# Four modulation rows computed among the first convolutions, and six buffers for the weight quantising

## The reference, cut to what matters

```
mod = (silu(c) @ wmod).reshape(1, 6, 1, 512)
sa, ca, ga, sb, cb, gb = six vectors of 512
ga = sign(ga) * max(|ga|, 0.25);  gb = the same of gb
h  = layernorm(x) * (1 + ca) + sa
x  = x + ga * mamba(h)          # W_in 2048x512, conv of 4 taps, silu, scan over 8192 tokens, 16 states, W_out 512x1024
h  = layernorm(x) * (1 + cb) + sb
x  = x + gb * ffn(h)            # gate, up 1408x512, down 512x1408; weights and inputs in blocks of 16, FP4
```

## Time and profile before

| what | us |
|---|---|
| median of 3 runs (5562.43 to 5564.1) | 5562.72 |
| the profiled execution's own time | 5563.82 |
| its span | 5561.9 |
| busy in the span: PE, DVE | 4831.9, 4961.6 |
| busy in the span: POOL, ACT | 4007.7, 3027.0 |
| end of setup (start of the Mamba block) | 51.13 |
| start of the first scan | 182.80 |

### The profile page before, as it was taken

One profiled execution on the slowest core, in us unless ns is written; L12 is line 12 of the kernel. 1 busy time (PEld: TensorE's weight loads), 2 busy tenths in 40 slices (PEclk: granted clock), 3 DMA queues, 4 the chain that ended last, 5 costly groups with the idle time before them and its releaser, 6 DMA issues. The chain is left out here.

```text
span 5561.9 us, 76495 instructions
## 1 busy us (share of the span) xinstructions
PE 4831.9 (87%) x21860; PEld 3350.4 (60%) x21860; DVE 4961.6 (89%) x4365; ACT 3027.0 (54%) x6492; POOL 4007.7 (72%) x1968
## 2 busy tenths in 40 slices
PE   6688897888978879888897888975799999999999
PEld 3355555455545545545554555554688888888887
DVE  6899999999999999999999999998688888888887
ACT  1677677777777767777677777764211111111111
POOL 4899999999999999999999999998122222222221
PEclk8799999999999999999999999997899999999999
DMA  5455564555545555455565656544210110101100
GB/s 200 155 189 167 179 195 160 189 173 180 191 156 190 176 170 197 159 189 169 178 195 154 193 172 181 184 154 133 93 34 28 34 33 29 34 29 34 34 28 27
DMA packets 398953, 745.63 MB, mean 134 GB/s; under 512 B 44563, under 2 KB 44691, under 8 KB 398454
## 3 DMA queue, kind: packets, MB, share of 16 engines
q1 hardware_dynamic: 394230, 724.19, 40.1%
q0 software_dynamic: 4352, 17.30, 0.9%
HBM read 698.06 MB, written 43.26 MB: 133 GB/s over the span
## 5 line engine op out<-in xcount | busy, mean ns | idle before, releaser
L644 POOL TENSOR_TENSOR slot<-du,b_row 128x1024 f32<-128x1024 f32 x1024 | 2401.4, 2371 | 50.3 <-PE y_ps L1064 45.9
L948 DVE TENSOR_TENSOR_SCAN decays<-decays,state,slot 128x1024 f32<-128x1024 f32 x592 | 1388.5, 2346 | 54.7 <-ACT slot L820 53.3
L811 ACT ACTIVATE decays<-delta,rate 128x512 f32<-128x512 f32 x2048 | 1326.3, 679 | 32.3 <-issue 9.5
L1064 PEld LDWEIGHTS y_ps<-ident,slot 128*128 128x128 f32 x8192 | 1004.9, 149 | 327.5 <-issue 214.0
L1064 PE MATMUL y_ps<-ident,slot 128*128 128x128 f32 x8192 | 1096.2, 287 | 82.2 <-POOL slot L651 78.7
L948 DVE TENSOR_TENSOR_SCAN slot<-decays,state,slot 128x1024 f32<-128x1024 f32 x432 | 1011.5, 2341 | 71.6 <-ACT slot L820 69.7
L651 POOL TENSOR_TENSOR slot<-slot,c_row 128x1024 f32<-128x1024 f32 x432 | 1023.9, 2370 | 69.8 <-ACT state L798 68.2
L1314 POOL TENSOR_TENSOR hq<-hid,qinv 128x1408 f32<-128x1408 f32 x64 | 165.9, 2593 | 1220.5 <-DVE qinv L1340 1220.5
L1004 PE MATMUL work_ps<-h_t,win 128*128 128x512 f32 x2048 | 1000.8, 635 | 35.2 <-DVE delta L874 18.6
L954 DVE TENSOR_TENSOR slot<-decays,c_row 128x1024 f32<-128x1024 f32 x592 | 724.0, 1223 | 56.9 <-DVE decays L948 4.2
L1279 ACT ACTIVATE act_gate<-gate_ps 128x512 f32<-128x512 f32 (+1 forms) x192 | 108.2, 563 | 1136.7 <-PE gate_ps L1421 612.5
(11 more groups left out here) (193 smaller groups left out, 7424.5 us busy)
## 6 DMA issues: line engine op xcount, KB each, us to landing
b_row<-b_c_rows SPq DMA_DIRECT2D x1024, 256.0 KB, 3.8
c_row<-b_c_rows SPq DMA_DIRECT2D x1024, 256.0 KB, 3.6
win<-in_w_in SPq DMA_DIRECT2D x256, 256.0 KB, 4.4
xt<-in_x SPq DMA_DIRECT2D x16, 1024.0 KB, 7.4
xr<-in_x SPq DMA_DIRECT2D x64, 256.0 KB, 4.3
x_after_mamba<-xr SPq DMA_DIRECT2D x64, 256.0 KB, 4.1
xa<-x_after_mamba SPq DMA_DIRECT2D x64, 256.0 KB, 2.8
xres<-x_after_mamba SPq DMA_DIRECT2D x64, 256.0 KB, 2.6
```

The lines of the kernel that those rows point to most:

```text
L644: pool.tensor_tensor(slot[:, u % SLOTS, :, :], du[:, p % 2, :, :], two(b_row[:, u % BC_RING, :]), ALU.mult).then_inc(S["ub_ready"], 1)
L811: act.activation(decay[u % 2][:, i, :], delta[:, p % 2, i, :], ACT.Exp, scale=rate[:, 2 * p + i, n:n + 1]).then_inc(S["decay_ready"], 1)
L948: dve.tensor_tensor_scan(d if u in DVE_C else h, d, h, state[:, 2 * p, n:n + 1], ALU.mult, ALU.add).then_inc(S["scan_done"], 1)
L1064: op = pe.matmul(y_ps[i][:, s, :], slot[:, u % SLOTS, i, s * P:(s + 1) * P], ident[:, :], is_transpose=True, start=False, stop=(n == N - 1 ...
```

## The change

The setup keeps only what the first LayerNorm and the projections need: a third of `wmod`, the two column vectors, `diag`, `rate`, `wdt`. `xc`, which held nothing before the block began, is allocated earlier and its second half serves as home of the rows. The other four modulation vectors are computed in chunk -1 of the Mamba block: SP loads their parts of `w_mod` into buffers that are not in use yet (`delta`, `b_row`, `c_row`, `du`) and `wout` behind them; PE does one 512-column matmul of a row product after each of the 16 `i` and `c` pieces, ACT copies each finished row out after the fourth, eighth, twelfth and sixteenth piece, and DVE makes the signed rows inside `prepare()`, before groups 4 and after group 9. The column of `gb` is made by four small matmuls on PE in place of the way through HBM. `wout` is multiplied by `ga` on POOL at the end of `prepare()`, in four instructions of 1024 elements a partition. The first two groups of feed-forward weights are loaded at the Mamba block's start and the next four at the start of `prepare()`; the ring has six buffers, the two new ones in `zs`.

```diff
-    PREP_RING = SLOTS // 2
+    PREP_RING = SLOTS // 2 + 2
...
-                wmod = ssb("wmod", [P, KT, 6 * DM])
+                wmod = ssb("wmod", [P, KT, 2 * DM])
...
-                LOADS += [(mod_loaded[i], wmod[:, :, pairs[i]], w_mod[:, :, pairs[i]]) for i in range(3)]
+                LOADS += [(mod_loaded, wmod[:, :, :], w_mod[:, :, 0:2 * DM])]
...
-                        pool.wait_ge(mod_loaded[2], 16)
-                        for g in range(PREP_RING):
-                            prep_load(pool, g)
...
-                        for j in range(NB):
-                            dve.tensor_tensor(wout[:, j, :], wout[:, j, :], ga_mag[:, :], ALU.mult)
...
+            VECTORS = (("gate", 5, delta[:, :, :, :].rearrange("p a b t -> p (a b) t")), ("shift", 3, b_row[:, :, :]),
+                       ("scale", 4, c_row[:, :, :]), ("mix", 2, du[:, :, :, :].rearrange("p a b t -> p (a b) t")))
...
+                    load_vector(0)
+                    for i in range(WIN_RING):
+                        load_win(i, Chunk(None, 0))
+                    for i in range(1, len(VECTORS)):
+                        load_vector(i)
+                    sp.dma_start(wout[:, :, :], w_out).then_inc(wout_loaded, 16)
                     all_chunks(sp, body)
...
                     def prepare():
+                        for g in range(2, PREP_RING):
+                            prep_load(pool, g)
                         for g in range(len(PREP) + 1):
...
+                        pool.wait_ge(wout_loaded, 16)
+                        pool.wait_ge(mix_row, 1)
+                        for j in range(0, NB, 2):
+                            pool.tensor_tensor(wout[:, j:j + 2, :], wout[:, j:j + 2, :],
+                                               mix_mag.unsqueeze(1).to_broadcast((P, 2, DM)), ALU.mult).then_inc(wout_done, 1)
...
                     def conv_out(j, c):
                         b = BANK["c", j]
+                        if j == 0 and c.reg is None and c.off == 1:
+                            act.wait_ge(mod_saved, 16)
+                            act.wait_ge(wout_done, PAIRS)
...
+                        elif j == 0:
+                            for g in (SLOTS // 2, SLOTS // 2 + 1):
+                                act.wait_ge(prep_saved[g], prep_count(g))
...
+                    def row_out(i):
+
+                        src = y_ps[1][:, :, :].rearrange("p s q -> p (s q)")
+                        act.wait_ge(rows_done, i + 1)
...
+                            mag, raw_row = (gate_mag, gate_raw) if name == "gate" else (mix_mag, mix_raw)
+                            act.activation(mag, src, ACT.Abs)
+                            act.activation(raw_row, src, ACT.Copy).then_inc(rows_out, 1)
...
+                    def signed(mag, raw_row, i):
...
+                        dve.tensor_scalar(mag, mag, 0.25, None, ALU.max).then_inc(own, 1)
+                        chain(dve.tensor_scalar(raw_row, raw_row, 0.0, 2.0, ALU.is_ge, ALU.mult), 2)
+                        return dve.scalar_tensor_tensor(mag, raw_row, -1.0, mag, ALU.add, ALU.mult)
...
                         for g in range(len(PREP) + 1):
+                            if g == 4:
+                                dve.wait_ge(rows_out, 1)
+                                signed(gate_mag, gate_raw, 0).then_inc(gate_row, 1)
+                            if g == len(PREP):
+                                dve.wait_ge(rows_out, 4)
+                                signed(mix_mag, mix_raw, 1).then_inc(mix_row, 1)
...
+                    def row_mm(i, k):
+                        if k == 0:
+                            wait(pe, rows_out, i)
+                            pe.wait_ge(vec_loaded[i], 16)
+                        if i == 2 and k == 0:
+                            pe.wait_ge(gate_row, 1)
+                            for m in range(KT):
+                                op = pe.matmul(y_ps[1][:, 0, m:m + 1], gate_mag[0:1, m * P:(m + 1) * P], one[0:1, 0:1],
+                                               start=True, stop=True)
+                            op.then_inc(col_done, 1)
+                            pe.wait_ge(col_out, 1)
+                        op = pe.matmul(y_ps[1][:, :, :].rearrange("p s q -> p (s q)"), c_wide[:, k, :], VECTORS[i][2][:, k, :],
+                                       start=(k == 0), stop=(k == KT - 1))
```

More of the change, by code:

```diff
@@ L174, in adaln_block @@
     bc_rows = nc.dram_tensor("b_c_rows", (L // T * 2 * N, T), F32, kind="Internal").ap()
[L175 removed]
+    mod_rows = nc.dram_tensor("ffn_modulation", (2, DM), F32, kind="Internal").ap()
     F = w_gate.shape[0]
@@ L340, in _ @@
                         last.then_inc(cols_ready, 1)
-                        for i in range(4):
-                            if i % 2 == 0:
-                                pe.wait_ge(mod_loaded[1 + i // 2], 16)
-                            for k in range(KT):
-                                last = pe.matmul(rows_ps[i][:, :], c_wide[:, k, :],
-                                                 wmod[:, k, (2 + i) * DM:(3 + i) * DM],
-                                                 start=(k == 0), stop=(k == KT - 1))
-                        last.then_inc(rows_ready, 1)
                     @block.vector
@@ L401, in adaln_block @@
             sp_e = sb("sp_e", [P, T])
+            slot = sb("slot", [P, SLOTS, 2, T])
             b_row = sb("b_row", [P, BC_RING, T])
@@ L421, in adaln_block, with prep_width, prep_rows, prep_count @@
             prep_inv = [sb(f"prep_inv{i}", [P, 2 * 2 * T // QB]) for i in range(2)]
+            def prep_width(g):
+                return sum(n * w.shape[1] for w, _, _, n, _ in PREP[g])
+            def prep_rows(g):
+                b = g % PREP_RING
+                if b < SLOTS // 2:
+                    return slot[:, 2 * b:2 * b + 2, :, :].rearrange("p a b t -> p (a b t)")
+                b -= SLOTS // 2
+                return zs[:, 4 * b:4 * b + 4, :].rearrange("p a t -> p (a t)")
+            def prep_count(g):
+                return 16 * sum(len(PREP[i]) for i in range(g % PREP_RING, g + 1, PREP_RING))
+            def prep_load(pool, g):
+                for w, _, row, n, col in PREP[g]:
+                    m = w.shape[1]
+                    pool.dma_start(prep_rows(g)[:, col:col + n * m].rearrange("p (a d) -> p a d", a=n),
+                                   w[row * P:(row + n) * P, :].rearrange("(a p) d -> p a d", p=P)).then_inc(prep_loaded[g % PREP_RING], 16)
+            VECTORS = (("gate", 5, delta[:, :, :, :].rearrange("p a b t -> p (a b) t")), ("shift", 3, b_row[:, :, :]),
+                       ("scale", 4, c_row[:, :, :]), ("mix", 2, du[:, :, :, :].rearrange("p a b t -> p (a b) t")))
             ps = lambda name, shape: mamba.enter_context(nc.psum_tensor(name, shape, F32))
@@ L438, in adaln_block @@
             xr_saved = [sem(f"xr_saved{i}") for i in range(TILES)]
-            gb_loaded, prep_scales, prep_scaled, prep_rounding, prep_rounded, prep_quant = (
-                sem("gb_loaded"), sem("prep_scales"), sem("prep_scaled"), sem("prep_rounding"), sem("prep_rounded"),
+            vec_loaded = [sem(f"vec_loaded{i}") for i in range(len(VECTORS))]
+            wout_loaded, rows_done, rows_out, gate_row, col_done, col_out, own, mix_row, wout_done, mod_saved = (
+                sem("wout_loaded"), sem("rows_done"), sem("rows_out"), sem("gate_row"), sem("col_done"), sem("col_out"),
+                sem("own"), sem("mix_row"), sem("wout_done"), sem("mod_saved"))
+            prep_scales, prep_scaled, prep_rounding, prep_rounded, prep_quant = (
+                sem("prep_scales"), sem("prep_scaled"), sem("prep_rounding"), sem("prep_rounded"),
                 sem("prep_quant"))
@@ L545, in load_b @@
                         src = row(u % N, c)
+                        if u == 0 and c.reg is None and c.off == 0:
+                            sp.wait_ge(rows_done, 4)
                         if u == 0:
@@ L667, in _ @@
                         pool.memset(const[:, i, :], v).then_inc(S["cleared"], 1)
+                    for g in range(2):
+                        prep_load(pool, g)
                     pool.wait_ge(S["cleared"], 8)
@@ L785, in lead_exp, with col_of_gate @@
                         act.activation(first, huge[:, :], ACT.Copy).then_inc(S["lead_cut"], 1)
+                    def row_out(i):
+                        src = y_ps[1][:, :, :].rearrange("p s q -> p (s q)")
+                        act.wait_ge(rows_done, i + 1)
+                        name = VECTORS[i][0]
+                        if name == "shift":
+                            act.activation(ffn_rows[:, 0, :], src, ACT.Copy).then_inc(rows_out, 1)
+                        elif name == "scale":
+                            act.activation(ffn_rows[:, 1, :], src, ACT.Identity, bias=one[:, 0:1]).then_inc(rows_out, 1)
+                        else:
+                            mag, raw_row = (gate_mag, gate_raw) if name == "gate" else (mix_mag, mix_raw)
```

(5 more changed lines are left out.)

95 lines of the change are left out of this document (40 added, 55 removed).

## The result

| | kernel before | changed kernel |
|---|---|---|
| median of 5 runs, us | 5563.07 (5562.43 to 5564.1) | 5535.97 (5532.19 to 5538.6) |
| the profiled execution: time, span | 5563.82, 5561.9 | 5535.97, 5534.1 |
| start of the Mamba block | 51.13 | 24.51 |
| `x_low` | 163.95 | 148.35 |
| start of the first scan | 182.80 | 166.99 |

The ratio is 0.995 (95% interval 0.9935 to 0.9964). The direction was right and the size was not. Single executions of one kernel lie apart too, those of the changed kernel by 6.4 us, and a profile is of one execution.

The account below looks back on a forecast made before the run. Only the time ahead of the first scan could move, with DVE and POOL's quantising chain last there. −26.2 + 5 − 3.2 + 5 + 4 + 0.2 = −15.2 us gave 5547.5 us, range 5538 to 5555.

Parts of the forecast that it names:

- T: Start of the Mamba block, at the end of setup: from 51.13 to 24.9, a term of −26.2 us.
- `x_low`: DVE's row ending the quantising chain, forecast at T + 123.6 (T + 112.8 before), still later than PE and ACT's chain.
- First scan: End of the preparing stretch: first scan forecast at 167.5 instead of 182.80, the span ending the same 15 us earlier.
- `signed`: Signed rows on DVE inside `prepare()`: one of three instructions waits for POOL's whole product each time, +5 and +4 us.
- Rival A: Signed rows on DVE: no clash with POOL's product, 1.5 us each; −21.2 us in all, 5541.5; chance 0.15.
- rival C: PE's pieces in the preparing stretch: PE stays at the lower clock, 1.2 GHz; +28 us, 5590; chance 0.04.
- First loads: At the block's start: groups 0 and 1, now loaded by POOL only then, arrive late for DVE; +5 us, bounds 1 and 10.
- Six buffers: In the quantising: group 4 is loaded early, so its wait goes, −3.2 us; waits at groups 6, 7 and 9 stay.
- The PE and ACT chain: Beside the quantising: grows 8.5 us to T + 113.4, costing nothing as DVE's chain stays last with 10 us in hand.
- So the time can move only ahead of the first scan: Repeating part: its scan's instructions, order and waits are unchanged, so the first scan's shift reaches the end one for one.
- a sign of being wrong: Forecast wrong if the first scan moves by less than 11 or more than 20 us, or the span does not follow.
- Rival D: Repeating part: different rhythm (`slot`'s address, earlier first chunk), 0.3% either way, or an unseen wait; about 5562; chance 0.06.

Follow-up runs that it names:

- run 4: Changed kernel with a ring of four buffers instead of six: 31.1 us below the kernel before, ratio 0.9945.
- run 5: Changed kernel, same six buffers, loads issued four groups ahead instead of two: 5522.54 us, 41.5 below the kernel before, ratio 0.9923.
- run 7: Kernel of run 5 with both signed rows made on POOL: 43.1 us below the kernel before (0.9923); with 64 ACT copies added, 41.1 (0.9926).
- Runs 1 and 2: 1: kernel before with seven ACT copies 5551.5 us, changed kernel with 121 5550.02; 2: changed kernel with 128 copies 0.9948, kernel before with seven POOL memsets 0.9999.
- run 3: Changed kernel with `slot` allocated ahead of the setup's tiles as before: 33.8 us below the kernel before, ratio 0.9943.

## Why the prediction was wrong

**What held.** The steps up to the first scan came out one by one. T: 24.9 forecast, 24.51 measured. `x_low`: T + 123.6 and T + 123.8. `du` behind `x_low`: 13.1 and 12.87. First scan: 167.5 and 166.99. `signed`: +5 and +4, measured 4.9 and 3.9 (72.36 to 77.24; 0.42 + 2.81 + 0.69 = 3.9). Rival A, no clash, is out with that. So is rival C: only the first piece of PE ran long (5.78 us, and 6.39 before), the second took 3.70 and no later one more, and between 48 and 131 us PE's granted clock was 1.00, the level of 2.4 GHz.

**Terms that were off and cancelled.** *First loads*: +5 forecast; the first peaks waited 6.66 + 0.57 us, and the second peak stood 6.8 us further behind T than before (14.87 against 8.0). The estimate of 6 by the equal turns of the Trainium skill (DMA: Bandwidth & Descriptors, Queues, rings and completion order) was nearer. *Six buffers*: -3.2 forecast, and the wait at group 4 did go, but run 4 shows that the ring was not the cause; it was covered by the signed row. The waits for groups 6 to 9 moved: 3.89 at group 6 and 2.16 at group 8, none at 7 and 9, together 6.05 us where the kernel before had 7.03. So what the first loads cost beyond their term came back in part in these waits and in the signed rows' few tenths. That `x_low` came out within 0.2 us is luck as far as these go.

**A term that was far off and cost nothing.** The PE and ACT chain was to grow by 8.5 us, to T + 113.4. It ends at T + 107.2, 2.3 more than before. A row product takes 1.02 us, but mostly in time in which PE waited for ACT's copy anyway. That left 16.6 us in hand rather than 10, which is why run 5 could gain 9.5. How hard that edge is, run 7 shows.

**The step that failed.** "So the time can move only ahead of the first scan, at 182.80, and a shift of the first scan should come out at the end one for one." The first scan moved by 15.8 us and the span by 27.8; the prediction had named that as a sign of being wrong. The premise was that unchanged instructions in an unchanged order keep their time. Runs 1 and 2 show that they do not: the 7 instructions by which ACT's code ahead of the loop had grown took away a second wait behind each jump, 1.8 to 2.2 us a time. The three kernels with ACT's code at the old place in the period have it at all five back edges and take 3682.6 to 3687.8 us from the first to the last scan; the eleven others never have it and take 3665.6 to 3678.8. That it is a wait for code is argued from the transfers and from the period, not seen in the record of the pause itself. In the groups of ACT this is 10.4 us, 32.3 against 21.9; seven instructions that do nothing give the kernel before 8.7 of the 12.4 us between first and last scan. Rival D came nearest, "a slightly different rhythm ... either way", at 0.06, but it put the cause in the address of `slot`, which run 3 rules out, and priced it at the whole gain. What stays open is the rest of about 3.7 us between 8.7 and 12.4, and with it what spreads the eleven kernels without the pause over 13 us; some other part of the rhythm moves too, as rival D had it.

**Was it to be seen?** The page of before had it: 9.5 us of "issue" ahead of a group that has no reason to wait. What that pause hangs on could not be read from one trace. What could have been done is to give a cause that shifts code a range of its own; by these runs some 10 us to either side.

## What to carry to other kernels

Where a kernel loops, count an edit's instructions ahead of the loop too: compare the "issue" idle time of each engine's groups before and after, and before crediting or blaming an edit for a change of some tenths of a per cent, shift the code by a few useless instructions, and by several different numbers of them, and measure again. When buffers are added, issue the loads further ahead as well: here the ring alone gave nothing and the ring with the distance 9.5 us at the first scan. And a signed row or another small DVE instruction with operands and result in SBUF can last, where it falls beside one of POOL's, as long as that one and not what its own size says; moving it to POOL helps only if what waits for it has that time.

## What the runs showed of the hardware

- A taken jump costs ACT 2.7 to 4.8 us of "issue" at this loop, and 1.8 to 2.3 us more where the code ahead of it is shifted by -7 or 121 instructions from the changed kernel's; shifts by 0, 64 and 128 are free of the second pause. Seven memsets on POOL change nothing.
- DVE's `scalar_tensor_tensor` with two SBUF operands is held beside POOL (4.05 and 2.96 us against 0.69), and so is its `tensor_tensor` (1.9 us each against 0.61). On POOL the steps of a signed row took 1.50 to 1.95 us (`tensor_scalar`) and 1.27 us (`tensor_tensor`), on DVE 0.42 and 0.69 undisturbed.
- With 4.2 MB on POOL's queue a block was left 5.2 us later, about when they had landed; whether that was the reason was not tested.
